# A two-layer graph kernel: the adjacency handed over with its axes swapped, a second PSUM bank for r and z, and a new order of the matmul engine's work

## The reference, cut to what matters

```python
h = relu(layernorm(x))
# layer 0
x_conv = relu(bn(conv17(relu(bn(conv1(h))))) + h)
s = h @ w_se.T + b_se;  A = exp(-|s_n - s_m|^2) * adj
x_nmp = A @ relu(h @ w_msg.T + b_msg)
gi = concat(x_conv, x_nmp) @ w_ih.T + b_ih;  gh = h @ w_hh.T + b_hh
r, z = sigmoid(gi_r + gh_r), sigmoid(gi_z + gh_z)
x = x + (1 - z) * tanh(gi_n + r * gh_n) + z * h
# layer 1
h = relu(layernorm(x))
x = x + relu(h @ W[:256] + (adj @ h) @ W[256:] + bias)
```

## Time and profile before

| what | value |
|---|---|
| median of 3 runs | 2043.64 us (2042.54 to 2045.88) |
| the profiled execution: its time, its span | 2046.88 us, 2045.1 us |
| PE busy | 1910.9 us (93% of the span) |
| PEld busy | 1440.8 us (70%) |
| DVE busy | 1486.3 us (73%) |
| ACT busy | 798.1 us (39%) |
| POOL busy | 378.7 us (19%) |
| first and last transpose of an adjacency | 648.8 us, 2002.7 us |

### The profile page before, as it was taken

One profiled execution on the slowest core, in us unless ns is written; L12 is line 12 of the kernel. 1 busy time (PEld: TensorE's weight loads), 2 busy tenths in 40 slices (PEclk: granted clock), 3 DMA queues, 4 the chain that ended last, 5 costly groups with the idle time before them and its releaser, 6 DMA issues.

```text
span 2045.1 us, 37541 instructions
## 1 busy us (share of the span) xinstructions
PE 1910.9 (93%) x13020; PEld 1440.8 (70%) x13020; DVE 1486.3 (73%) x3296; ACT 798.1 (39%) x1480; POOL 378.7 (19%) x554
## 2 busy tenths in 40 slices
PE   2877989999975999999999999999999999999997
PEld 2666767764434777777777777777777777877775
DVE  3977878852234777877777778777777787777775
ACT  3854445544224333333333333333333333333332
POOL 1021111100011222121221222212212222122120
PEclk9989999999987999999999999999999999999998
DMA  3076565656234222222322223223222232232220
GB/s 109 1 283 232 184 226 196 198 212 257 98 139 146 68 85 68 93 77 72 98 68 85 85 68 96 73 73 97 68 90 80 68 100 70 75 95 68 91 79 16
DMA packets 162857, 224.40 MB, mean 110 GB/s; under 512 B 15863, under 2 KB 112878, under 8 KB 162030
## 3 DMA queue, kind: packets, MB, share of 16 engines
q1 hardware_dynamic: 159550, 223.35, 32.7%
q10 hardware_dynamic: 3248, 0.27, 0.1%
HBM read 133.39 MB, written 90.18 MB: 109 GB/s over the span
## 4 chain that ended last, share of the span: by engine, by line
PE 63%; DVE 3%; ACT 2%; issue 0%; DMA 0%; ACTq 0%; POOLq 0%; POOL 0%; DVEq 0%
PE ps_rz L1291 26%; PE ps_n L1291 13%; PE ps_l L1291 13%; PE ps_b L1291 9%; DVE nmp L1397 2%; ACT nmp L1392 2%; PE ps_adj L1317 1%; PE ps_d L1300 1%; DMA rows<-spectra 0%; ACTq L1213 0%; PE ps_s L1251 0%; PE ps_d L1515 0%; DVE out_sum L1567 0%; DVE out_sb L1571 0%; DVE update L1480 0%
## 5 line engine op out<-in xcount | busy, mean ns | idle before, releaser
L1446 ACT ACTIVATE tanh_rz<-sum_rz,w_scale 128x512 f32<-128x512 f32 x128 | 92.7, 724 | 473.8 <-DVE sum_rz L1437 473.8
L882 PE MATMUL m_ps<-big 128*128 128x512 f16 (+1 forms) x1152 | 268.5, 376 | 4.1 <-DVE ysb L792 2.1
L1291 PE MATMUL ps_rz<-w_ih,nmp 128*128 128x512 f32 x768 | 206.6, 404 | 11.4 <-DVE nmp L1397 11.3
L1471 POOL TENSOR_TENSOR x_new<-xin,new 128x256 f32<-128x256 f32 x128 | 93.5, 731 | 663.5 <-ACT new L1464 663.5
L1291 PE MATMUL ps_rz<-w_ih,conv_t 128*128 128x512 f32 x768 | 209.1, 407 | 0.0
L882 PEld LDWEIGHTS m_ps<-big 128*128 128x128 f16 x1152 | 112.4, 98 | 108.5 <-DVE ysb L792 3.6
L1291 PE MATMUL ps_rz<-w_hh,ht 128*128 128x512 f16 x768 | 186.8, 379 | 0.9 <-DVE sum_n L1440 0.9
L1291 PE MATMUL ps_l<-w_l,h2t 128*128 128x512 f16 x768 | 179.4, 384 | 1.4 <-DVE h2t L1527 1.4
L1291 PEld LDWEIGHTS ps_rz<-w_ih,nmp 128*128 128x128 f32 x768 | 134.7, 188 | 51.1 <-DVE nmp L1397 26.6
L792 DVE SCALAR_TENSOR_TENSOR ysb<-m_ps,ysb 128x512 f16<-128x512 f32 x96 | 66.1, 689 | 118.5 <-ACT ysb L718 118.5
L1291 PEld LDWEIGHTS ps_rz<-w_ih,conv_t 128*128 128x128 f32 x768 | 134.8, 189 | 23.8
(11 more groups left out here) (219 smaller groups left out, 3814.7 us busy)
## 6 DMA issues: line engine op xcount, KB each, us to landing
xin<-in_x SPq DMA_DIRECT2D x128, 256.0 KB, 2.9
spectra<-ysb SPq DMA_DIRECT2D x96, 256.0 KB, 2.0
rows<-spectra SPq DMA_DIRECT2D x64, 384.0 KB, 3.5
x_normed<-xhat SPq DMA_DIRECT2D x64, 256.0 KB, 3.3
h_turned<-ht SPq DMA_DIRECT2D x64, 256.0 KB, 2.4
adj_in<-in_adj SPq DMA_DIRECT2D x64, 256.0 KB, 3.7
ht<-h_turned SPq DMA_DIRECT2D x64, 256.0 KB, 3.3
xhat<-x_normed SPq DMA_DIRECT2D x64, 256.0 KB, 2.9
```

Source lines behind the costliest of these rows:

```text
L882: last = pe.matmul(dest, x_, w_, start=n == 0, stop=n == 11, skip_group_check=True)
L1291: last = pe.matmul(dest, stationary(dl), moving(wl), start=start and n == 0, stop=stop and n == 2, **kw)
L1446: act.activation(tanh_rz[:, i, :], sum_rz[:, i, :], ACT.Tanh, scale=w["scale"][:, 4:5]).then_inc(S["rz_tanh"], 1)
L1471: pool.tensor_tensor(x_new[:, i, :], xin[:, p, i, :], new[:, i, :], ALU.add).then_inc(S["x_new_done"], 1)
```

## The change: what it does

The host hands every graph's adjacency over transposed. The transfer moves the same number of bytes into the same tile `adj_in`, which now holds what `ps_adj` held. `turn_adj` goes away; ACT and DVE read `adj_in` in SBUF instead of the bank. SP loads the next adjacency into a buffer once `att_done` and `adj_low` of two graphs before are there, instead of `adj_turned`.

The freed bank becomes a second one for r and z, one for each half. `gates_first` is cut into three functions, and PE's list gets another order. The lists of DVE, ACT, POOL and SP stay as they were.

```diff
-    adj_d = adj.rearrange("g (t p) m -> g p t m", p=P)
+    adj_d = adj.rearrange("g (m p) n -> g p m n", p=P)
...
-        ps_adj = ps("ps_adj")
-        ps_rz = ps("ps_rz")
+        ps_rz = [ps(f"ps_rz{i}") for i in range(H)]
...
-            act.activation(adj_t[:, p, 0, :, :].rearrange("p h n -> p (h n)"), ps_adj[:, :],
-                           ACT.Copy).then_inc(S["adj_high"], 1)
+            act.activation(adj_t[:, p, 0, :, :], adj_in[:, p, :, :], ACT.Copy).then_inc(S["adj_high"], 1)
...
-            dve.tensor_tensor(adj_t[:, p, 1, :, :].rearrange("p h n -> p (h n)"), ps_adj[:, :],
-                              adj_t[:, p, 0, :, :].rearrange("p h n -> p (h n)").bitcast(F32),
+            dve.tensor_tensor(adj_t[:, p, 1, :, :], adj_in[:, p, :, :], adj_t[:, p, 0, :, :].bitcast(F32),
                               ALU.subtract).then_inc(S["adj_low"], 1)
...
-            dve.tensor_tensor(att[:, :, :].rearrange("p h n -> p (h n)"),
-                              ps_adj[:, :], expd[:, :, :].rearrange("p h n -> p (h n)"),
-                              ALU.mult).then_inc(S["att_done"], 1)
+            dve.tensor_tensor(att[:, :, :], adj_in[:, p, :, :], expd[:, :, :], ALU.mult).then_inc(S["att_done"], 1)
...
-        def gates_first(pe, t, p, i):
-
-            ready(pe, "rz_added", t, i, H)
+        def first_h(pe, t, p, i):
+
+            before(pe, "rz_added", t, H)
+            for kh in range(H):
+                three(pe, ps_rz[i][:, :], lambda s: ht[:, p, s, kh, i * P:i * P + P],
+                      lambda s: w["hh"][:, s, kh, 0:2 * D], kh == 0, False)
             ready(pe, "n_added", t, i, H)
...
                     if cur:
-                        turn_adj(pe, t, p)
                         distances(pe, t, p)
                         messages(pe, t, p)
-                        gates_first(pe, t, p, 0)
+                        first_h(pe, t, p, 0)
+                        first_conv_rz(pe, t, p, 0)
                         weighted(pe, t, p)
+                        first_conv_n(pe, t, p, 0)
                     if nxt:
                         inverse(pe, t + 1, 1 - p)
+                    if cur:
+                        gates_second(pe, t, p, 0)
                     if prev:
                         turn2(pe, t - 1, 1 - p, cur)
                     if cur:
-                        gates_second(pe, t, p, 0)
+                        first_h(pe, t, p, 1)
                     if prev:
                         layer1(pe, t - 1, 1 - p)
                     if cur:
-                        gates_first(pe, t, p, 1)
+                        first_conv_rz(pe, t, p, 1)
+                        first_conv_n(pe, t, p, 1)
                     if prev:
                         neighbours(pe, t - 1, 1 - p)
```

More of the change, by code:

```diff
@@ L1228, in load_rows @@
             sp.dma_start(rows[:, p, :, :, :].rearrange("p k l o -> p k (l o)"), rows_d[t]).then_inc(conv_loaded[p], 16)
-            before(sp, "adj_turned", t, 1, 2)
+            before(sp, "att_done", t, 1, 2)
+            before(sp, "adj_low", t, 1, 2)
             sp.dma_start(adj_in[:, p, :, :], adj_d[t]).then_inc(adj_loaded[p], 16)
@@ L1308, in exponential @@
                            scale=2.0).then_inc(S["exp_done"], 1)
[L1311 to L1319, removed]
         def adj_split_high(act, t, p):
-            ready(act, "adj_turned", t)
+            arrived(act, adj_loaded, t, p)
             before(act, "out_done", t, H, 2)
-            act.activation(adj_t[:, p, 0, :, :].rearrange("p h n -> p (h n)"), ps_adj[:, :],
-                           ACT.Copy).then_inc(S["adj_high"], 1)
+            act.activation(adj_t[:, p, 0, :, :], adj_in[:, p, :, :], ACT.Copy).then_inc(S["adj_high"], 1)
         def adj_split_low(dve, t, p):
             ready(dve, "adj_high", t)
-            dve.tensor_tensor(adj_t[:, p, 1, :, :].rearrange("p h n -> p (h n)"), ps_adj[:, :],
-                              adj_t[:, p, 0, :, :].rearrange("p h n -> p (h n)").bitcast(F32),
+            dve.tensor_tensor(adj_t[:, p, 1, :, :], adj_in[:, p, :, :], adj_t[:, p, 0, :, :].bitcast(F32),
                               ALU.subtract).then_inc(S["adj_low"], 1)
@@ L1411, in gates_first, with first_conv_rz @@
                       lambda s: w["hh"][:, s, kh, 2 * D:3 * D], kh == 0, False, skip_group_check=True)
+        def first_conv_rz(pe, t, p, i):
             if i == 0:
@@ L1414, in gates_first, with first_conv_n @@
             for kh in range(H):
-                three(pe, ps_rz[:, :], lambda s: conv_t[:, p, s, kh, i * P:i * P + P],
+                three(pe, ps_rz[i][:, :], lambda s: conv_t[:, p, s, kh, i * P:i * P + P],
                       lambda s: w["ih"][:, s, kh, 0:2 * D], False, False)
+        def first_conv_n(pe, t, p, i):
             for kh in range(H):
@@ L1425, in gates_second @@
             for kh in range(H):
-                last = three(pe, ps_rz[:, :], lambda s: nmp[:, s, kh, i * P:i * P + P],
+                last = three(pe, ps_rz[i][:, :], lambda s: nmp[:, s, kh, i * P:i * P + P],
                              lambda s: w["ih"][:, s, 2 + kh, 0:2 * D], False, kh == H - 1)
@@ L1436, in gate_sums @@
             before(dve, "rz_tanh", t, H)
-            dve.tensor_tensor(sum_rz[:, i, :], ps_rz[:, :], w["bias_rz"][:, :], ALU.add).then_inc(S["rz_added"], 1)
+            dve.tensor_tensor(sum_rz[:, i, :], ps_rz[i][:, :], w["bias_rz"][:, :], ALU.add).then_inc(S["rz_added"], 1)
             ready(dve, "n_done", t, i + 1, H)
@@ L1785 @@
     for name, value in inputs.items():
-        value = np.ascontiguousarray(value)
+        value = np.ascontiguousarray(value.transpose(0, 2, 1) if name == "adj" else value)
         short = name.replace("L0_gnn_", "").replace("L1_gnn_weight", "l1_w").replace("L1_gnn_bias", "l1_b")
```

6 lines of the change are left out of this document (2 added, 4 removed).

## The result

The changed kernel takes 2200.71 us, the median of 4 runs (2199.96 to 2208.57), against 2043.36 us for the kernel before in the same measurement. The ratio is 1.0777, with a 95% interval of 1.075 to 1.0803. It is slower by 157 us. The forecast was 2202 us.

A forecast was written before the change was run, and what follows sets the result against it. PE was taken as the bound, busy 980.97 of 989 us, with DVE's list nearly level. Slots grow from 21.51 to 24.03 us; 63 x 2.52 = 159 us more gives 2206 us profiled, 2202 us median, range 2150 to 2232 us.

The forecast's parts named there:

- Two new waits on PE: PE idles ahead of `weighted` for DVE's `msg`, some 1.3 us, and ahead of half 1's n part for `sum_n`, some 1.5.
- `turn2` as the large term: `turn2` behind `gates_second(0)` makes DVE's `h2t` and sums late: they need 3.26 us, PE has 1.74 of work, waiting 1.52.
- The walk round the slot: Step-by-step sum from `sum_rz` of half 1 to the next one: 24.03 us where a slot took 21.51.
- The lock term: POOL's `rstd_b` held by DVE's `adj_t` over SBUF, delaying `gates_second(0)` by 0.17 to 0.36 us; 0.27 taken.
- the one place in the trace of before where such a pair meets: POOL's `diff` and DVE's `x_new`, both reading SBUF: said to be the trace's only meeting, `x_new` ending 0.58 us behind.
- From slots to the whole: Slots 1 to 63 each 2.52 us longer: 159 us more over the kernel.
- DVE ends the slot, not PE: At the slot's end DVE's list finishes last, at 24.03 us against PE's 23.59, later by 0.44 us.
- The second bank takes away no wait: The second bank for r and z saves nothing, since `first_h(1)`'s place had no wait in the trace of before.
- The rival of the clock: Granted clock falls behind PE's two long waits, `weighted` and `layer1` run slower, slot 4.0 us longer: 2456 us; chance 0.03.
- The rival that PE closes up: PE's sum alone sets the slot, 20.71 us, 50 us less in all: 1993 us; chance 0.04.

The follow-up runs named there:

- e1: The changed kernel with only `turn2` moved back ahead of `gates_second(0)` in PE's list: 2088.5 us.
- e2: The changed kernel with DVE's sums of half 0 put ahead of its split of `turn2`: 2149.39 us.
- e7: The changed kernel with the n part of the convolution put back ahead of `weighted` on PE: 2203.39 us.
- e6: The changed kernel with DVE's `adj_split_low` moved behind `weighted_low`, away from POOL's `rstd_b`: 2192.59 us.
- e3: e2 with three further steps of DVE's list moved to fit PE's new order: 2071.31 us.
- e12: e8 with one bank for r and z again, the adjacency still handed over transposed: 2000.92 us.
- e5: The changed kernel with one bank for r and z instead of two: 2300.05 us.
- e9: The kernel before with PE's new order only: one bank, adjacency transposed on PE, both waits at the start of `first_h`: 2352.2 us.
- e8: e3 with ACT's reading of the inverse transform moved ahead of its split of `turn2`: 1999.48 us.
- e4: The changed kernel with PE's order as before, keeping the adjacency handed over transposed and two banks for r and z: 2048.82 us.
- e11: e10 with the wait for the n bank moved behind the r and z part: 2025.57 us.
- e10: The kernel before with e8's lists of PE, DVE and ACT; adjacency transposed on PE, one bank, both waits ahead of r and z: 2062.25 us.

## Why the prediction was right, point by point

- **Two new waits on PE.** Right in place and releaser, and near in size. The rows have 1.59 and 1.13 us by turns ahead of `weighted`, and 1.31 ahead of the n part of half 1, but the forecast was by starts. By starts (the block ahead of `weighted` takes 1.47 us where nothing waits) they are 1.76 and 1.29 us, where 1.31 was forecast. The n part starts 3.21 us behind `turn2` (1300.06 to 1303.27), against 3.26 in the walk. e1 and e2 each took the second wait away, from PE's side and from DVE's, and e7 showed what the n part has to do with the first.
- **`turn2` as the large term.** Right: DVE idle 3.53 us ahead of `h2t` (3 to 4 forecast), and putting `turn2` back recovers 112 of the 157 us.
- **The walk round the slot**, in us, came out step by step. Where the two slots of a pass differ, both are given:

| step | forecast | measured |
|---|---|---|
| `sum_rz` of half 1 to `weighted` | 6.26 | 6.48, 6.27 |
| `weighted` itself | 1.55 | 1.53 |
| its end to `gates_second(0)` | 1.92 | 1.80 |
| `gates_second(0)` | 2.23 | 2.21 |
| `turn2` to the n part of half 1 | 3.26 | 3.21 |
| the n part and `layer1` | 3.17 | 3.07 |
| `layer1`'s end to `u_s` | 0.70 | 0.80 |
| `u_s` to the last `out_sb` | 4.60 | 4.59 |
| the last `out_sb` to the next `sum_rz` | 0.34 | 0.60, 0.35 |
| the whole | 24.03 | 24.03, 24.08 |

- **The lock term was mis-sized.** I took 0.27 us from a range of 0.17 to 0.36. `rstd_b` was held exactly as said (0.55 us instead of 0.19), but `gates_second(0)` started 1.80 us behind `weighted`'s end (1320.34 to 1322.14) against 1.65 before, so the term is 0.15, and e6 gave back 0.15. The Trainium skill's page SBUF — State Buffer, Who interferes with whom, says that a DVE instruction with two SBUF inputs contends with a GpSimd instruction that reads SBUF, and that the one that issues first keeps the shared ports for its whole length. The rows above agree, in both directions: `pre_n` took 1.26 us beside `conv_v` and ended 0.28 us behind it. Of that second direction I had put 0.3 us into the range and nothing into the sum. Here this did no harm: DVE stood idle for 2.02 us ahead of `u_s` behind it.
- **A reading that was wrong.** I called the one place in the trace of before where such a pair meets. There is one in each slot, on DVE's side, between my own:

```profile
1304.84 1.16 POOL L1273 TENSOR_TENSOR conv_v<-conv_x,ht 128x512 f32<-128x512 f32 x1
1305.27 1.01 DVE L1454 SCALAR_TENSOR_TENSOR reset<-tanh_rz,sum_n 128x256 f32<-128x256 f32 x1
```

`reset` takes 1.01 us there instead of 0.43 and ends 0.28 us behind `conv_v`. So the handover did not bring DVE and POOL together for the first time. The term of the forecast is untouched, since DVE idled behind it before as well (0.84 us ahead of `u_s`). But this meeting, grown to two instructions, is a part of what held e3 back, and the trace of before could have warned of it.
- **A term that I left out** took its place: DVE's `sum_rz` starts 0.60 us after the last `out_sb` in every second slot (1311.73 to 1312.33) and 0.35 in the others, and in that same slot `att` starts 0.21 us later behind `sum_rz`. That is 0.23 us a slot in the mean. The slot in question is the first of a loop pass. The lock term was 0.12 too large, the n part with `layer1` 0.10, and four other steps 0.10 together; against that stand this 0.23 and `u_s`, put 0.10 too early. The errors cancel, and that is luck: the total was nearer than its terms.
- **From slots to the whole.** 62 slots of 2.54 us more (663.33 to 2153.89 us, against 669.98 to 2002.79) are 158 us, as forecast. The two profiled spans are only 153 us apart, since in the kernel before everything ahead of these slots took 6.7 us longer in that execution, and what follows them is 2 us longer in the changed one; the medians differ by 157.
- **DVE ends the slot, not PE:** right, `sum_rz` had no wait for PE.
- **The second bank takes away no wait:** right for the kernel before and for e12. In the new order with DVE's list unmoved it does shorten one, as e5 shows.
- **The rival of the clock** was nearer than 0.03 made it. In the changed kernel the clock stayed at 1.00 behind waits of 1.59 and 1.31 us. One move of DVE's (e2, waits of 1.90 us) or the loss of the bank (e5, 2.01 us) brought it down. The rival's price was too high: it wanted 4.0 us in every slot, and the falls of e2 and e9 took 1.3 to 1.7 us in some. I had weighed that waits are short and the slot mostly busy, and both were so in e2 as well.
- **The rival that PE closes up** gave 20.71 us a slot. The order does allow it: e8 has 20.83. It took DVE's and ACT's lists moved along with PE's. The Trainium skill's page Perfetto Trace Analysis, Optimizing Tensor Performance, would have banks rotated for this; by e8 and e12, with 1999.48 and 2000.92 us, the rotation is no part of the gain.

Whether the clock would also fall in e5 and e9 without the longer wait was not tried. Why the first slot of a pass has `sum_rz` 0.25 us late, and `att` 0.23 us behind `expd`'s end where the other has 0.03, stays open.

## What to carry to other kernels

When engines work through fixed lists, a block moved on one engine has to be followed along its results: each engine that reads it has its own list, and the old place in that list becomes the new wait. Here the changed kernel stood at +157 us against the kernel before with PE's list alone reordered, at +28 with DVE's list matched to it, and at -44 with two steps of ACT's list exchanged as well. Taking work off the engine that looks 99% busy brings nothing while another list runs level with it (e4), and 25 of the 28 us that it costs once that list has slack (e12 against e11). A wait should stand at the first instruction that needs it: one wait in front of a block that didn't need it cost 37 us (e10 against e11).

## What the hardware showed that I had not expected

- The granted clock fell to 0.50 behind waits of PE of 1.90 us (e2), 2.01 us (e5) and 2.70 us (e9), in some slots and not in others with the same wait in the record, and the block behind the wait then took up to 2.70 us instead of 1.69, or 2.41 instead of 1.46. A slot with a fall was 1.3 us longer in e2 and 1.6 to 1.7 us in e9 than one of its kind without. Behind the 1.59 us waits of the changed kernel it did not fall in any slot. What decides between two slots that look alike, these runs don't show.
- A DVE instruction of 0.42 us (`pre_n`, two inputs in SBUF) took 1.26 us beside POOL's `conv_v`, and `reset` 0.97 us beside `conv_x`: on the path that sets the end, meetings like these cost more than the instruction.
- The four transposes take 0.44 us of PE by their rows, but removing them from a closed-up slot gave 0.37 us in the mean (21.20 to 20.83). Every slot of e11 has 21.21 us. Those of e12 have 20.77, the full 0.44 less, and 20.90 by turns; in the longer ones, the first of a pass, PE's weight loads wait for `msg`, and `weighted` takes 1.54 us by starts (1316.70 to 1318.24) against 1.44 in e11 (1313.27 to 1314.71).
